# Batch 0 of a modulated attention block in another order: low parts ahead of powers, row tile 1 turned first, component loads moved up

## What is computed

```python
mod = (_silu(c) @ wmod).reshape(4, 6, 1, -1)
sa, ca, ga, sb, cb, gb = (mod[:, i] for i in range(6))
ga, gb = (sign(g) * max(|g|, 0.25) for g in (ga, gb))        # sign(0) = 1
h = layernorm(x) * (1 + ca) + sa
x = x + ga * attn(h)      # layernorm, QKV, rotary on K and V,
                          # A = 0.5 * sum_s cos_sim(K) * cos_sim(V) + 0.5, (A * Q) @ W_out + b_out, + h
h = layernorm(x) * (1 + cb) + sb
x = x + gb * ffn(h)       # relu(h W_up.T) W_down.T + (sum of the two top router weights) * h W_expert
```

## Time and profile before

| | |
|---|---|
| median of 3 runs | 369.16 us (368.67 to 369.51) |
| profiled execution | 368.55 us |
| its span, first to last instruction | 366.5 us |
| PE, DVE, ACT, POOL busy | 95%, 67%, 45%, 34% of the span |
| mean granted TensorE clock | 0.991 |
| moved by transfers | 27.45 MB |

### The profile page before, as it was taken

One profiled execution on the slowest core, in us unless ns is written; L12 is line 12 of the kernel. 1 busy time (PEld: TensorE's weight loads), 2 busy tenths in 40 slices (PEclk: granted clock), 3 DMA queues, 4 the chain that ended last, 5 costly groups with the idle time before them and its releaser, 6 DMA issues.

```text
span 366.5 us, 4921 instructions
## 1 busy us (share of the span) xinstructions
PE 349.9 (95%) x1776; PEld 286.7 (78%) x1776; DVE 244.8 (67%) x501; ACT 165.7 (45%) x317; POOL 123.4 (34%) x128
## 2 busy tenths in 40 slices
PE   4779799999999999999999999999999999999996
PEld 2238387878888788888888898988988898889885
DVE  2788989868978588785878459338722862382374
ACT  1476976884249701476017673335144423441110
POOL 0285766985823259232451232900100010000000
PEclk9969999999999999999999999999999999999999
DMA  6989567420030001000000003101200110011003
GB/s 211 389 328 307 241 232 247 168 103 2 1 86 2 0 0 31 0 1 2 0 29 2 0 2 114 30 2 43 74 0 0 59 57 2 0 59 58 2 0 115
DMA packets 10968, 27.45 MB, mean 75 GB/s; under 512 B 1200, under 2 KB 1584, under 8 KB 9792
## 3 DMA queue, kind: packets, MB, share of 16 engines
q1 hardware_dynamic: 10944, 27.13, 21.3%
HBM read 22.90 MB, written 4.23 MB: 74 GB/s over the span
## 4 chain that ended last, share of the span: by engine, by line
PE 80%; DVE 7%; DMA 4%; issue 3%; ACT 2%; POOL 2%; SPq 1%; POOLq 0%; DVEq 0%
PE ps L1191 25%; PE ps L1193 25%; PE ps L1192 25%; PE ps L1245 3%; DMA stage<-in_wmod 3%; DMA xs<-in_X 2%; DVE hst L795 1%; ACT z L601 1%; POOL w_lo L400 1%; PE ps L1216 1%; DVE acc L855 1%; DVE hst L789 0%; SPq L284 0%; POOL hrs L397 0%; DVE hb L1140 0%
## 5 line engine op out<-in xcount | busy, mean ns | idle before, releaser
L1191 PE MATMUL ps<-wv_hi,t_hi 128*128 128x260 f32 (+1 forms) x192 | 61.5, 321 | 0.4 <-ACT v_sb L640 0.4
L1193 PE MATMUL ps<-wv_hi,t_lo 128*128 128x260 f32 (+1 forms) x192 | 61.5, 320 | 0.0
L1192 PE MATMUL ps<-wv_lo,t_hi 128*128 128x260 f32 (+1 forms) x192 | 61.4, 320 | 0.0
L1191 PE MATMUL ps<-t_hi,w_hi 128*128 128x512 f32 x128 | 50.7, 396 | 0.8 <-DVE sb_col L1059 0.8
L1191 PE MATMUL ps<-w_hi,g_hi 128*128 128x512 f32 (+1 forms) x132 | 51.3, 389 | 0.0
L1193 PE MATMUL ps<-w_hi,g_lo 128*128 128x512 f32 (+1 forms) x132 | 50.6, 384 | 0.0
L1192 PE MATMUL ps<-w_lo,g_hi 128*128 128x512 f32 (+1 forms) x132 | 50.6, 383 | 0.0
L1193 PE MATMUL ps<-t_hi,w_lo 128*128 128x512 f32 x128 | 50.1, 391 | 0.0
L1192 PE MATMUL ps<-t_lo,w_hi 128*128 128x512 f32 x128 | 50.0, 390 | 0.0
L1191 PEld LDWEIGHTS ps<-wv_hi,t_hi 128*128 128x128 f32 x192 | 36.2, 189 | 3.8 <-issue 0.8
L1193 PEld LDWEIGHTS ps<-wv_hi,t_lo 128*128 128x128 f32 x192 | 36.1, 188 | 2.9
(11 more groups left out here) (151 smaller groups left out, 713.2 us busy)
## 6 DMA issues: line engine op xcount, KB each, us to landing
stage<-in_w SPq DMA_DIRECT2D x4, 1024.0 KB, 6.4
out<-xs SPq DMA_DIRECT2D x15, 256.0 KB, 2.0
xs<-in_X SPq DMA_DIRECT2D x3, 1024.0 KB, 8.9
xs<-in_wmod SPq DMA_DIRECT2D x8, 256.0 KB, 5.5
stage<-in_w SPq DMA_DIRECT2D x8, 256.0 KB, 8.3
stage<-in_wmod SPq DMA_DIRECT2D x2, 1024.0 KB, 9.7
gate_bc<-mod_rows SPq DMA_DIRECT2D x8, 256.0 KB, 3.4
xs<-in_X SPq DMA_DIRECT2D x2, 512.0 KB, 6.8
```

What stands on the lines that cost most here:

```text
L1191: mm(dst, l_hi, r_hi, start=start, stop=False)
L1192: mm(dst, l_hi, r_lo, start=False, stop=False)
L1193: return mm(dst, l_lo, r_hi, start=False, stop=stop)
```

## The change

The change reorders batch 0's work on all five engines and moves some buffers. It adds and removes no arithmetic.

- POOL: `rstd_x0(1)` goes behind `low_kv(0, 0)` and `shift_h0(0)`; `rstd_x(1)` goes ahead of `shift_h0(3)`; `scale_rows(1, 3)` behind `weight(0, 1)`; `rstd_h(1, 2, 2)` ahead of `weight(0, 2)`.
- TensorE: row tile 1 is turned right behind `mod_pair((2, 3))`, row tile 2 inside `kv_tile(0, 0)`, row tile 3 behind `mod_rest`.
- ScalarE: `t0_evac(2)`, `norm_sums(0, 0)` and batch 1's first two tiles come ahead of `normalise(0, 3, 1)`; batch 1's fourth tile comes behind `t0_evac(3)`; Q's high part behind the copies of the component bank; `normalise(1, 2, 2)` ahead of `x_squares(2)`.
- VectorE: `t0_split(0)` comes ahead of row tile 3's scaling, `t0_split(1)` ahead of batch 1's statistics, row tile 3's own statistics behind `kv_rows(0, 0)`, `t0_split(3)` behind `kv_products(0, 1)`, `kv_rows(0, 2)` behind batch 1's last statistics, `x_mean(2)` behind `h_shift(1, 2, 2)`.
- SP and buffers: component 4 goes to `x_slot(3)` and is loaded right behind the broadcasts, component 3 goes to `stage`'s first half, Q's weights to its second, the component bank's copies to `x_slot(3)`; `load_x(3)` no longer waits for Q's low parts; the first `load_modulation` no longer waits on `h1_s`.

```diff
-        mod_raw, mod_abs, mod_sign, gate_rows = (stage[:, 1, i * D:(i + 1) * D] for i in range(4))
+        mod_raw, mod_abs, mod_sign, gate_rows = (xs[:, (3 * NT + i) * D:(3 * NT + i + 1) * D] for i in range(4))
...
-        MODS = ((2, x_slot(2)), (5, gate_bc[:]), (4, stage[:, 0, :]), (3, stage[:, 1, :]))
+        MODS = ((2, x_slot(2)), (5, gate_bc[:]), (4, x_slot(3)), (3, stage[:, 0, :]))
...
-        w_raw = (stage[:, 0, :], stage[:, 1, :], x_slot(3), stage[:, 0, :], stage[:, 1, :], stage[:, 0, :], stage[:, 1, :])
+        w_raw = (stage[:, 0, :], stage[:, 1, :], stage[:, 1, :], stage[:, 0, :], stage[:, 1, :], stage[:, 0, :], stage[:, 1, :])
...
-                sp.wait_ge(h1_s, b * NT)
+                if b > 1:
+                    sp.wait_ge(h1_s, b * NT)
...
             sp.wait_ge(row_out, 32)
             load_modulation(1)
+            load_component(2)
             sp.wait_ge(wlo_k, NC)
-            sp.dma_start(MODS[2][1], wmod[MODS[2][0]]).then_inc(wm_in[MODS[2][0]], 16)
+            load_component(3)
             sp.wait_ge(wlo_v, NC)
-            sp.dma_start(MODS[3][1], wmod[MODS[3][0]]).then_inc(wm_in[MODS[3][0]], 16)
...
+            sp.wait_ge(modt_ps, 1)
+            load_x(3)
             sp.wait_ge(wlo_q, NC)
-            load_x(3)
-            sp.wait_ge(modt_ps, 1)
...
-                if b == 0:
-                    rstd_x(1)
                 weight(b, 0)
                 if b == 0:
-                    for t in range(NT):
-                        scale_rows(1, t)
+                    scale_rows(1, 0)
+                    scale_rows(1, 1)
+                    scale_rows(1, 2)
                     weight(b, 1)
+                    scale_rows(1, 3)
                     rstd_h(1, 0, 2)
                     for k in range(NC):
                         low_q(k)
+                    rstd_h(1, 2, 2)
                     weight(b, 2)
-                    rstd_h(1, 2, 2)
...
             rstd_x0(0)
-            rstd_x0(1)
             low_kv(0, 0)
             shift_h0(0)
+            rstd_x0(1)
             low_kv(1, 0)
...
             low_kv(1, 1)
-            shift_h0(3)
             low_kv(0, 2)
             low_kv(0, 3)
+            rstd_x(1)
+            shift_h0(3)
...
             def first_attention():
-                norm_sums(0, 0)
-                normalise_x(1)
-                t0_evac(2)
+                norm_sums(0, 1)
                 t0_evac(3)
-                norm_sums(0, 1)
-                split_hi(2)
+                normalise_x1(3)
                 act.wait_ge(mod_ps, 2)
                 nc.scalar.activation(mod_abs, ps[:, MOD_BANK, :], ACT.Abs, scale=2.0).then_inc(abs_s, 1)
                 act.wait_ge(abs_s, 1)
                 nc.scalar.activation(mod_raw, ps[:, MOD_BANK, :], ACT.Copy).then_inc(mod_row_s, 1)
+                split_hi(2)
                 normalise(1, 0, 2)
                 x_sums(2)
                 norm_sums(0, 2)
+                normalise(1, 2, 2)
                 x_squares(2)
-                normalise(1, 2, 2)
...
             t0_evac(1)
+            t0_evac(2)
+            norm_sums(0, 0)
+            normalise_x1(0)
+            normalise_x1(1)
             normalise(0, 3, 1)
+            normalise_x1(2)
...
             def first_attention():
-                x_stats(1)
-                t0_split(1)
-                x_aggr(1)
                 dve.wait_ge(const_in, 32)
                 dve.wait_ge(row_out, 32)
                 kv_rows(0, 0)
                 x_shift(1)
+                h_stats(0, 3)
+                h_aggr0(3)
+                t0_split(2)
                 kv_products(0, 0)
                 kv_sum(0, 0)
                 h_row(1, 0)
                 kv_rows(0, 1)
-                t0_split(2)
                 h_row(1, 1)
-                t0_split(3)
                 h_stats(1, 0)
                 h_stats(1, 1)
                 h_aggr(1, 0, 2)
                 kv_products(0, 1)
+                t0_split(3)
                 h_shift(1, 0, 2)
                 kv_sum(0, 1)
-                kv_rows(0, 2)
                 mod_gates()
                 h_row(1, 2)
                 h_row(1, 3)
-                x_mean(2)
                 h_stats(1, 2)
                 h_stats(1, 3)
                 h_aggr(1, 2, 2)
+                kv_rows(0, 2)
+                h_shift(1, 2, 2)
+                x_mean(2)
                 kv_products(0, 2)
-                h_shift(1, 2, 2)
                 kv_sum(0, 2)
                 mod_cols()
...
+            h_aggr0(2)
+            t0_split(0)
+            scale_row0(3)
+            h_row0(3)
             split_lo_kv(1, 2)
             split_lo_kv(1, 3)
+            t0_split(1)
+            x_stats(1)
+            x_aggr(1)
             first_attention()
...
                     if b == 0 and t == 0 and k == 1:
-                        transposes0(1)
-                    if b == 0 and t == 1 and k == 2:
-                        transposes0(3)
+                        transposes0(2)
...
                     if b == 0 and t == 1:
                         mod_rest()
+                        transposes0(3)
...
             transposes0(0)
             mod_pair((2, 3))
+            transposes0(1)
```

More of the change, by code:

```diff
@@ L318, in load_gate_b, with load_component @@
                              mod_rows[ROW_GB, b:b + 1, :].to_broadcast([P, D])).then_inc(gb_in[b], 16)
-            sp.dma_start(MODS[1][1], wmod[MODS[1][0]]).then_inc(wm_in[MODS[1][0]], 16)
+            def load_component(i):
+                comp, weights = MODS[i]
+                sp.dma_start(weights, wmod[comp]).then_inc(wm_in[comp], 16)
+            load_component(1)
             sp.wait_ge(mod_sb, 1)
@@ L323, in _ @@
             sp.dma_start(mod_rows[ROW_SA], rows[32:32 + B, :]).then_inc(row_out, 16)
-            sp.dma_start(MODS[0][1], wmod[MODS[0][0]]).then_inc(wm_in[MODS[0][0]], 16)
+            load_component(0)
             sp.wait_ge(row_out, 32)
             load_modulation(1)
+            load_component(2)
             sp.wait_ge(wlo_k, NC)
-            sp.dma_start(MODS[2][1], wmod[MODS[2][0]]).then_inc(wm_in[MODS[2][0]], 16)
+            load_component(3)
             sp.wait_ge(wlo_v, NC)
-            sp.dma_start(MODS[3][1], wmod[MODS[3][0]]).then_inc(wm_in[MODS[3][0]], 16)
             sp.dma_start(w_raw[2], w[2]).then_inc(w_in[2], 16)
@@ L584, in x_squares, with normalise_x1 @@
                                          accum_out=xss[:, t:t + 1]).then_inc(xsum_s, 1)
+            def normalise_x1(t):
+                act.wait_ge(t_ps, t + 1)
+                act.wait_ge(xnm_s, 1)
+                nc.scalar.activation(z[:, t, :], xs[:, tok(1, t)], ACT.Identity, bias=xnm[:, t:t + 1],
+                                     scale=xrs[:, t:t + 1]).then_inc(xn_s, 1)
             def normalise_x(g):
-                wait(act, t_ps, g * NC if g > 1 else 0)
+                act.wait_ge(t_ps, g * NC)
                 act.wait_ge(xnm_s, g)
                 for t in range(NT):
-                    if g == 1:
-                        act.wait_ge(t_ps, t + 1)
                     nc.scalar.activation(z[:, t, :], xs[:, tok(g, t)], ACT.Identity, bias=xnm[:, t:t + 1],
@@ L1072, in _ @@
             h_aggr0(1)
-            for t in (2, 3):
-                scale_row0(t)
-                h_row0(t)
-                if t == 3:
-                    t0_split(0)
-                h_stats(0, t)
-                h_aggr0(t)
+            scale_row0(2)
+            h_row0(2)
+            h_stats(0, 2)
+            h_aggr0(2)
+            t0_split(0)
+            scale_row0(3)
+            h_row0(3)
             split_lo_kv(1, 2)
             split_lo_kv(1, 3)
+            t0_split(1)
+            x_stats(1)
+            x_aggr(1)
             first_attention()
@@ L1304, in attention @@
                     out_rows_of(b - 1)
-                else:
-                    transposes0(2)
                 for t in range(1, NT):
```

## The result

The changed kernel takes 373.66 us (median of 4 runs, 372.13 to 374.46) where the kernel before took 369.34 (4 runs, 368.67 to 370.56). The ratio is 1.0085, 95% interval 1.0049 to 1.0121: slower, by 3.1 us if taken from the ratio, 4.3 from the medians. The forecast was +1.6, and its range ended at 372.9. From the prediction's 369.16 the ratio gives 372.3, inside that range; the median of 373.66 lies beyond it. The profiled execution took 372.13 us, span 370.2; the other three ran at a mean granted clock of 0.982 in place of its 0.986, so the profile shows the kernel at its fastest, very likely with less time at half clock than the others had.

A forecast was written before the change was run, and what follows sets the result against it. TensorE was taken as the bound, busy 320.81 of 325.33 us from 41.17 us to the end. The terms -2.6 + 3.4 + 0.8 gave +1.6, a forecast of 370.8 us, range 368.0 to 372.9.

The forecast's parts named there:

- M: Start of `mod_rest` on TensorE: 41.20 us in the kernel before, forecast 38.6.
- term 2: From M to C: late turning of row tile 3 and VectorE's contention with POOL cost +3.4 us (+1.2 to +4.5).
- C: Start of the second Q chunk on TensorE: 60.18 us before, M + 18.98; forecast M + 22.4.
- rival 4: TensorE's clock falls to half in the longer gap ahead of `mod_rest`: 3.4 us on top, 374.2 us; chance 0.09.
- half clock behind 38: Sign of being wrong: TensorE at half clock after 38 us, which would point to rival 4.
- the wait for `a_col`: Sign of being right: TensorE waits for `a_col` behind C, with 0.4 us of slack used up.
- Term 1: Front of batch 0: earlier row tiles and component loads move M by -2.6 us (-3.2 to -1.9).
- M follows `mod_sb` directly: Front of batch 0: argument for a faster outcome, 367.4 us, chance 0.15; `mod_sb` was forecast 2.6 us earlier.
- The wait for POOL at M + 9: Sign of being right: on VectorE, `h_shift(1,0,2)` waits for POOL until about 9 us after M.
- Term 3: Behind C: late squares and `x_mean(2)` delay `a_col` and the V product, +0.8 us (0 to 1.3).
- the wait for `sb_col`: Sign of being right: TensorE waits 2 to 4 us for `sb_col` ahead of C, until M + 22.

The follow-up runs named there:

- e2: Kernel before with only POOL's second power moved behind K's first low part and first shift: 368.93 us, ratio 0.9964.
- e8: Changed kernel with twelve unused products ahead of `mod_rest` and nine more ahead of the wait for `sb_col`: 372.00 us, ratio 1.0074.
- e4: Changed kernel with Q's low parts computed in one column of 512 each, leaving out nearly all of `low_q`: 370.72 us, ratio 1.0008.
- e12: e8 with the squares ahead of batch 1's last normalised tiles and `x_mean(2)` ahead of the statistics of tiles 2 and 3: 371.93 us, ratio 1.0065.
- e9: e6 with VectorE's and ScalarE's order between M and C put back as in the kernel before: 367.83 us, ratio 0.9951.
- e1: Changed kernel with row tile 3 turned ahead of `mod_rest` instead of behind it: 368.72 us, ratio 0.9957.
- e5: Changed kernel with component 4's load put back behind SP's wait for `wlo_k`: 374.21 us, ratio 1.0106.
- e7: e2 plus POOL's shift of row tile 3 moved behind K's last low parts, nothing else of the change: 368.44 us, ratio 0.9947.
- e10: e9 without the twelve unused products ahead of `mod_rest`: 369.07 us, ratio 0.9976.
- e3: Changed kernel with twelve unused products ahead of `mod_rest`, to fill TensorE's idle gap: 372.19 us, ratio 1.0071.
- e6: e1 with twelve unused products behind row tile 3's turning and ahead of `mod_rest`: 368.45 us, ratio 0.9949.

## Why the prediction was right, and where it was short

The verdict, slower, came for the reason given: M is won, more is lost behind it. The value is in the range by the ratio only, and partly by luck. Two of the three terms came out beyond their own bounds (term 2 at +4.72 with bounds +1.2 to +4.5, what lies behind C at +1.90 with 0 to 1.3), because of a cost that the sum left out, the clock; the range was wide enough for it, though it was set without rival 4. One of the signs of being wrong, half clock behind 38, did appear, and the wait for `a_col` named as a sign of being right did not. By its terms:

- **Term 1, right in size, wrong in one cause.** M 38.28, forecast 38.6; z0 17.59 (17.85), `rows` 22.74 (22.95), component 2 at 24.21 (24.45). The broadcasts did wait for the stores, until 26.81, where 25.3 would be as long behind the first store as before. That cost less than it might: the last load went out at 28.14, 2.1 us earlier than before, and landed 9.9 us behind its issue in place of 10.71, 2.9 earlier. What was wrong is the sentence that M follows `mod_sb` directly. By the chain of e2 it does not, as long as K's last low parts end at 29.8; it needs POOL's other move as well. The chain of waits of the kernel before shows this, one piece ahead of the earlier trace rows. The step read the load's 10.71 us and not the piece that released its issue. A second miss in the front did no harm: VectorE's two `wv_lo` took 3.40 us beside POOL, where they took 1.48; TensorE had no wait from there to `mod_rest`.
- **Term 2, right mechanism, 1.3 short.** Measured +4.72, forecast +3.4. Without the clock's 1.70 it is +3.0, and e8 measures the same, 21.98 - 18.98. The contention was 2.58 (2.19 and 0.39) by e4, and `kv_sum(0,2)` took 1.14 in place of 1.01: 2.7 in all, forecast 3.3. So the term missed the clock's 1.7 and was 0.4 too high in the rest. The wait for POOL at M + 9 came at M + 10.9, which is 9.2 and the clock's 1.7.
- **Term 3, right mechanism, hidden here and under-sized.** In e8, where the clock leaves it bare, it is 307.72 - 306.32 = +1.4, forecast +0.8 (to 1.3); e12, with the squares first, gives back 1.0 of it. In the changed kernel no wait for `a_col` is seen, since the clock makes TensorE later than it.
- **Rival 4 was not a rival but a term.** The clock did fall behind the gap of 3.41, at half the price (1.70 and not 3.4), and again behind the wait for `sb_col`, which the prediction itself had put at 2 to 4 us and for which it had set no price in clock. Net of what it hides, the clock is 1.7 + 0.5 of the 3.7 us between the profiled executions. The forecast left it out with a chance of 0.09. The earlier trace rows had shown a fall behind 3.60 us of idle, and the 3.7 us that the prediction itself put ahead of `mod_rest` lay at that length; the clock fell in five of the six kernels here that had a gap of 3.2 us or more there; the sixth is e2, with 3.51.

Not tried: a kernel that keeps M early and has neither the contention nor the late squares. e9 comes nearest.

## What to carry to other kernels

Before pricing an earlier input of a transfer, read the piece of the chain that released its issue; the queue's wait is often on another engine's list. A step that is moved to a later place brings its chain there, and the chain's cost is that of its new neighbours: two VectorE passes over SBUF that ran alone cost 2.2 us more beside POOL. And a new idle gap on the bounding engine is priced twice, as idle and as the clock behind it, but such prices overlap: what the clock makes late may hide the next wait.

## What the runs showed of the hardware

- The granted clock after an idle gap of TensorE. It fell to half (1.2 GHz) over `mod_rest` behind 3.41, 3.21, 3.4, 3.64 and 4.75 us of idle (changed kernel, e1, e4, e5, e7) and behind 2.12 (e10), but not behind 2.47, nor behind the 3.51 of e2, whose `mod_rest` ran at 1.00. It fell behind the 2.26 us ahead of C in the changed kernel and e3 and behind e5's 2.31, and not behind the 1.59 (e9), 1.55 (e6), 1.37 (e12) and 0.80. `mod_rest` then took 5.1 to 6.3 us in place of 3.57. The length of the gap alone does not settle it. Each of these is one execution, and executions of one kernel differ: e7's profiled one had a mean granted clock of 0.986, its other nine 0.990 to 0.995.
- A VectorE column operation with one SBUF input, 0.16 us alone, took 1.23 beside POOL (e12). The same section of the page SBUF — State Buffer of the Trainium skill says that VectorE's `tensor_scalar` can contend as well, when its operands let it enter a two-port mode. The row agrees with it; in which mode it ran, no row shows.
- The last component's load, 1 MB of `in_wmod`, took from 9.80 us (e10) to 12.98 (e7) from issue to landing.
